# Key products of two 512-column matmuls per channel chunk, with both PSUM banks for one half and the sum taken by VectorE into SBUF

## What is computed

```python
xn = group_norm(x)                                  # 32 groups, no affine part
q, k, v = split(xn_tokens @ qkv_w.T + qkv_b)        # 256 columns each
q = relu(q)
k = relu(k + pos_enc)                               # the part that the change touches
z  = 1 / (q . sum_over_tokens(k) + 1e-6)            # per head, 8 heads of 32
out = ((q @ (k.T @ v)) * z) @ proj_w.T + proj_b     # linear attention, per head
y = x + out
```

## Time and profile before

| | us |
|---|---|
| median of 3 executions | 2671.64 (2662.23 to 2674.28) |
| the profiled execution's own time | 2664.9 |
| its span, first to last instruction | 2663.1 |
| mean granted TensorE clock | 0.998 of full speed |

### The profile page before, as it was taken

The page is one execution under the profiler, slowest core; times in us unless marked ns, Lnnn a source line. Parts: engine busy times, 40 slices in busy tenths (PEclk is TensorE's granted clock), DMA queues, the critical chain, the costliest instruction groups (busy, mean ns, idle before and its releaser), DMA issues.

```text
span 2663.1 us, 45248 instructions
## 1 busy us (share of the span) xinstructions
PE 2595.4 (97%) x15812; PEld 2215.1 (83%) x15812; DVE 1590.4 (60%) x2500; ACT 1660.0 (62%) x2543; POOL 1955.2 (73%) x1217
## 2 busy tenths in 40 slices
PE   5999999999999999999999999999999999999997
PEld 4878888788888888888888888888888888888885
DVE  6646666566665565656566555566655666555546
ACT  4656666565666656666666665666666666665654
POOL 4758777686777867767687786877768687686875
PEclk9999999999999999999999999999999999999999
DMA  7557878787787878878788687887878788776769
GB/s 260 180 181 229 273 226 267 218 262 237 237 266 226 266 225 248 254 244 250 237 270 257 210 262 237 252 263 225 254 243 254 235 264 250 238 237 200 229 184 296
DMA packets 357472, 642.07 MB, mean 241 GB/s; under 512 B 34432, under 2 KB 55808, under 8 KB 357248
## 3 DMA queue, kind: packets, MB, share of 16 engines
q1 hardware_dynamic: 357248, 639.18, 77.3%
HBM read 519.25 MB, written 119.80 MB: 240 GB/s over the span
## 4 chain that ended last, share of the span: by engine, by line
PE 74%; DVE 6%; issue 6%; POOL 6%; ACT 4%; DMA 3%; SPq 1%; ACTq 0%; DVEq 0%; POOLq 0%
PE banks L549 17%; PE banks L573 16%; PE banks L605 15%; PE banks L561 11%; PE banks L563 5%; PE banks L540 5%; PE banks L590 3%; POOL kacc L1229 2%; POOL hl L1215 2%; DMA y<-xr 2%; ACT xn L1015 2%; DVE kk L840 1%; DVE banks L835 1%; DVE stats L819 1%; POOL posb L1236 1%
## 5 line engine op out<-in xcount | busy, mean ns | idle before, releaser
L1229 POOL TENSOR_TENSOR kacc<-kacc,kt 128x512 f32<-128x512 f32 x368 | 476.2, 1294 | 307.2 <-ACT kt L1044 304.9
L549 PE MATMUL banks<-wqk,hl 128*128 128x256 f32 x4608 | 646.1, 290 | 12.8 <-POOL hl L1215 12.7
L1215 POOL TENSOR_TENSOR hl<-xn,hl 128x512 fp32r<-128x512 f32 x384 | 494.6, 1309 | 207.5 <-ACT hl L1027 207.3
L825 DVE TENSOR_TENSOR xt<-banks,xt 128x512 fp32r<-128x512 f32 x400 | 274.5, 686 | 569.1 <-ACT xt L1032 568.9
L573 PE MATMUL banks<-hl,wqk 128*128 128x512 f32 x2304 | 600.7, 396 | 6.5 <-DVE xr L854 6.4
L549 PEld LDWEIGHTS banks<-wqk,hl 128*128 128x128 f32 x4608 | 575.6, 191 | 18.6 <-POOL hl L1215 18.6
L561 PE MATMUL banks<-kk,xt 128*128 128x512 f32 x1600 | 584.8, 400 | 3.6 <-DVE kk L840 3.6
L605 PE MATMUL banks<-uhl,mhl 128*128 128x512 f32 (+1 forms) x2316 | 541.7, 383 | 2.1 <-DVE xr L854 2.1
L1244 POOL TENSOR_TENSOR q<-q,zb 128x1024 f32<-128x1024 f32 x180 | 432.9, 2405 | 113.7 <-DMA zb<-z_rows 113.5
L605 PEld LDWEIGHTS banks<-uhl,mhl 128*128 128x128 f32 x2316 | 423.7, 188 | 89.8 <-issue 2.5
L573 PEld LDWEIGHTS banks<-hl,wqk 128*128 128x128 f32 x2304 | 406.3, 188 | 100.3 <-DVE xr L854 8.7
(11 more groups left out here) (117 smaller groups left out, 2374.2 us busy)
## 6 DMA issues: line engine op xcount, KB each, us to landing
posb<-pos_plus_bk SPq DMA_DIRECT2D x375, 256.0 KB, 5.7
xs<-in_x SPq DMA_DIRECT2D x184, 512.0 KB, 6.0
xa<-in_x SPq DMA_DIRECT2D x184, 512.0 KB, 6.4
xr<-in_x SPq DMA_DIRECT2D x184, 512.0 KB, 3.9
zb<-z_rows SPq DMA_DIRECT2D x736, 128.0 KB, 4.5
y<-xr SPq DMA_DIRECT2D x184, 512.0 KB, 7.2
z_rows<-zt SPq DMA_DIRECT2D x32, 256.0 KB, 5.5
posb<-in_pos SPq DMA_DIRECT2D x25, 256.0 KB, 4.2
```

Of the source, the lines that this page charges most:

```text
L549: last = mm(psK[:, par(n, h), i * C:(i + 1) * C], hl_of(t)[:, a, c, s:s + P], wqk[:, w, c, C:2 * C], start=(j == 0), stop=(j == len(terms) ...
L1215: g.tensor_tensor(hl_of(t)[:, 1, :, s], xn_of(n, t)[:, :, s], hl_of(t)[:, 0, :, s], ALU.subtract).then_inc(xl_ready, 1)
L1229: g.tensor_tensor(both, both, kt[:, par(n, h), :], ALU.add).then_inc(ks_done, 1)
```

## The change

The two key products that share a stationary operand (high x by high weights, high x by low weights) become one matmul: its moving operand is the high and the low weights of the keys side by side, 2 x 256 columns, and its output fills a whole bank. The third product (low x by high weights) is added into the bank's first 256 columns. Each of a half's two tiles so takes one bank, and a half takes both; the keys of a half therefore wait for `kt_ready` of the half before in place of `kr_ready` of the half two before. VectorE adds the bank's second part and the position into `kt`, and then the bank's first part to that, also into `kt`; the second addition waits for the first through the new semaphore `kp_ready`, the first waits for `ks_done` of the half two before, since `kt` is written earlier than it was. `key_high`, `key_low` and `key_keep` read `kt` in SBUF in place of PSUM, and `key_keep` works in place.

```diff
@@ transpose_and_k
-                wait(pe, kr_ready, half_no(n, h) - 2)
+                wait(pe, kt_ready, half_no(n, h) - 1)
                 for i in range(TILES):
                     s = tok + i * P
-                    terms = [(c, a, w) for c in range(CC) for a, w in ((0, 0), (0, 1), (1, 0))]
-                    for j, (c, a, w) in enumerate(terms):
-                        last = mm(psK[:, par(n, h), i * C:(i + 1) * C], hl_of(t)[:, a, c, s:s + P], wqk[:, w, c, C:2 * C],
-                                  start=(j == 0), stop=(j == len(terms) - 1))
+                    for c in range(CC):
+
+                        mm(psK[:, i, :].rearrange("p (w n) -> p w n", w=2), hl_of(t)[:, 0, c, s:s + P], wqk[:, :, c, C:2 * C],
+                           start=(c == 0), stop=False)
+                        last = mm(psK[:, i, 0:C], hl_of(t)[:, 1, c, s:s + P], wqk[:, 0, c, C:2 * C],
+                                  start=False, stop=(c == CC - 1))
@@ key_add
-                v.tensor_tensor(psK[:, par(n, h), :], psK[:, par(n, h), :], posb[:, s, :], ALU.add).then_inc(kt_ready, 1)
+                wait(dve, ks_done, half_no(n, h) - 2)
+                both = kt[:, par(n, h), :].rearrange("p (i n) -> p i n", i=TILES)
+                v.tensor_tensor(both, psK[:, :, C:2 * C], posb[:, s, :].rearrange("p (i n) -> p i n", i=TILES),
+                                ALU.add).then_inc(kp_ready, 1)
+                dve.wait_ge(kp_ready, half_no(n, h))
+                v.tensor_tensor(both, psK[:, :, 0:C], both, ALU.add).then_inc(kt_ready, 1)
@@ key_low
-                v.scalar_tensor_tensor(out=kk[:, hp, :, 1, :], in0=psK[:, hp, :].rearrange("p (i n) -> p i n", i=TILES),
+                v.scalar_tensor_tensor(out=kk[:, hp, :, 1, :], in0=kt[:, hp, :].rearrange("p (i n) -> p i n", i=TILES),
                                        scalar=0.0, in1=kk[:, hp, :, 0, :].bitcast(F32),
                                        op0=ALU.max, op1=ALU.subtract).then_inc(kl_ready, 1)
@@ key_high
-                a(kk[:, par(n, h), :, 0, :], psK[:, par(n, h), :].rearrange("p (i n) -> p i n", i=TILES),
+                a(kk[:, par(n, h), :, 0, :], kt[:, par(n, h), :].rearrange("p (i n) -> p i n", i=TILES),
                   ACT.Relu).then_inc(kh_ready, 1)
@@ key_keep
-                wait(act, ks_done, half_no(n, h) - 2)
                 act.wait_ge(kl_ready, half_no(n, h))
-                a(kt[:, par(n, h), :], psK[:, par(n, h), :], ACT.Relu).then_inc(kr_ready, 1)
+                a(kt[:, par(n, h), :], kt[:, par(n, h), :], ACT.Relu).then_inc(kr_ready, 1)
```

More of the change, by code:

```diff
@@ L139, in build @@
         xtl_ready = sem("xtl_ready")
+        kp_ready = sem("kp_ready")
         kt_ready = sem("kt_ready")
```

## The result

The changed kernel takes 3040.88 us (median of 4, 3035.64 to 3042.38) against 2670.45 us of the kernel before (median of 4): ratio 1.139, 95% interval 1.137 to 1.141. It is slower by 370 us. The forecast was 3089 us with a range of 2890 to 3345. The profiled execution took 3040.5 us, its span is 3038.5 us.

What follows compares the result with a forecast made beforehand. PE at 97% was taken as the bound, with the ACT-DVE loop 0.78 us behind in a 12.10 us step. Summed, 292 + 301 + 16 - 129 - 56 = 424 us on 2664.9 gave 3089 us, range 2890 to 3345.

Steps and rivals of the forecast that it cites:

- The loop: Closed chain of ACT's and DVE's in-order lists through one step: 12.10 us with 0.78 to spare, predicted to become 14.4.
- The second addition: On DVE, in the chain in both halves: 0.73 us each, 400 times, 292 us.
- The wait for POOL: Odd half's key_low, with two SBUF inputs, waits until POOL's u_low ends: 1.57 us, 192 times, 301 us.
- ACT's reads of SBUF: ACT's copies of 512 elements from SBUF instead of PSUM: 0.02 us more, 800 times, 16 us.
- The cover: Existing waits that absorb added time: ACT's 128.9 us for PE's queries, and 56 us at the 15 batch junctions.
- the two junction waits: Two operations at batch junctions waiting for PE, 62.0 and 44.9 us in all; 56 of the 107 were to absorb added time.
- PE, 36 us: Key matmuls on PE: a half's keys fall from 1.51 to 1.42 us, 0.09 less, 36 us for 400 halves.
- the first rival: PE stays the bound and gets faster, 2629 us, chance 0.04; or no change within 0.5%, chance 0.02.
- Signs: Expected in the trace: PE's share near 83%, 2.5 us of PE waiting a step, keys 1.42 us a half, steps 14.4 us.
- The addition alone: Rival: key_low does not wait for POOL, so only the second addition costs; 2811 us, chance 0.11.
- The wait in the even half: Rival: even half's key_low also waits, for POOL's scale, 250 us more; 3339 us, chance 0.08.

Runs made afterwards that it cites:

- e1_add: Kernel before with the addition of position and bias done twice in PSUM, the second waiting for the first; 2824.34 us, ratio 1.0577.
- e8_all: Changed kernel with POOL's scale and u_low waiting for key_low, statistics moved behind key_low, second query part's save moved behind x_high_t; 2792.59 us, ratio 1.0460.
- e2_sbuf: Kernel before with its one addition writing to kt in SBUF, which key_high, key_low and key_keep read; 2868.25 us, ratio 1.0744.
- e4_ulow: Changed kernel with POOL's u_low moved behind the key_sum of the odd half; 3044.06 us, ratio 1.1402.
- e6_gate: Changed kernel with two more POOL waits: scale for the even half's key_low, u_low for the odd half's; 2909.93 us, ratio 1.0899.
- e3_psum: Changed kernel with the sum written back to PSUM and read there, keys waiting for key_keep of the half before; 2932.63 us, ratio 1.0983.
- e5_mm: Kernel before with the new key matmuls alone, both tiles into the half's one bank, one addition, no new wait; 2651.84 us, ratio 0.9934.

## Why the prediction was right, and where its sizes were off

**The loop.** Right. PE was the bound by 0.78 us in 12.10, and the change put more than that on the chain of ACT and DVE beside it. The step came out at 14.29 for 14.43. That the chain is what counts is shown by e1_add (0.72 a step in each half, and no more than that, gives 12.82), and by e8_all, which shortens the chain to 11.86, keeps the additions, and has PE as the bound again in those steps.

**The second addition, 0.73 us.** 0.71 (1567.34 - 1566.63).

**The wait for POOL, 1.57 us in each odd half.** The mechanism, the half, the instruction of POOL and the 0.55 us behind its end are all as forecast, and e2_sbuf, e4_ulow and e6_gate show that it takes POOL's instruction and not the operands alone; e3_psum shows that it takes both inputs in SBUF. The size in sum was 301 us; `key_low`'s busy time grew by 400 x (1318 - 682) ns, 254 us (682 is its mean on the page of before). 165 of the 192 odd halves met `u_low`; those near junctions and in the first batch met other work or none, and 19 even halves waited that were to go free.

**ACT's reads of SBUF, 16 us.** 400 x (631 - 598) + 400 x (632 - 596) ns = 28 us, the means on both pages; the copy that I took for a measure was 0.614.

**The cover, 129 + 56 us.** ACT's query waits were used up but for 17.1 us. Of the two junction waits one fell by 42 us and the other not at all (44.9 and 47.3), and for the addition alone there was none (e1_add). With 0.71 x 400 = 284, 254 and 28 us added and 112 + 42 taken off the sum would be 412; 376 were measured between the two profiled executions. The 36 us between are not placed; some of `key_low`'s waits may lie outside the loop. That the sum came as near as 424 to 376 is in part luck: the wait for POOL was taken 47 us too high, while ACT's reads and the two covers together came out 43 us dearer than forecast.

**PE, 36 us.** This figure failed, though it is in the first rival's price and not in the sum, and the time did not hang on it. I took the gram for the model of the new keys; keys follow transposes, and the first matmul behind those costs 0.08 us more than the ones behind it, in both kernels. The whole gain is 17.8 us (e5_mm). The Trainium skill's spacing rule (TensorE: Matmul & The Clock Gate, Back-to-back issue gap) gave an estimate of 4 us; the measurement lies between the two.

**Signs.** PE's share was to be near 83% and is 88%, because its busy time rose from 2595.4 to 2672.4 us with 1600 fewer matmuls: the profile's matmuls overlap less when there are gaps between groups, and PE stands idle before 426 matmuls in place of 42. I should not have divided busy time by a new span. The step shown has 1.80 us of idle PE and not 2.5, 1.32 of it at the odd half's gram. The keys were to take 1.42 us a half and take 1.49. The rest of the signs came.

**The rivals.** PE did not stay the bound. The addition alone was to give 2811, and e1_add, which is that without ACT's 16 us, gives 2824. The wait in the even half came in 19 of 208 halves of the changed kernel, not as the rule; in e2_sbuf it came in 99 of them, in e4_ulow in 165.

## What to carry to other kernels

An engine at 97% is a bound only until the next chain is longer: before work is moved to an engine with 40% idle time, follow that engine's list through one full step, back to itself, and see how much of the period is waiting for the bound engine. Here that was 0.78 of 12.10 us, and the price was 1.4 us of additions plus a wait. And an operand moved from PSUM to SBUF can change who an instruction waits for: a VectorE instruction with two SBUF inputs here waited out whatever GpSimd had begun, so ask what that is at the moment when it comes.

## What was not expected of the hardware

POOL waits for DVE just as DVE waits for POOL: in e2_sbuf `u_low` takes 2.94 us in place of 2.39 when `key_low` begins 0.02 us ahead of it. So a collision avoided in one half was paid in the next, and the kernel with no second addition at all still lost 7.4%. And two added waits (e6_gate) made the kernel 131 us faster: `key_low` never got past a POOL instruction that had begun (191 times in the changed kernel), while one that has not begun can be held back at little cost.

A wait of PE can cost twice. In e8_all PE stands idle for 3.4 us at most junctions, and at 12 of the 14 its next matmuls then run longer, at a granted clock of 0.50 in the one shown; in the changed kernel it waits 0.8 to 0.9 us in the same place, and the six matmuls behind it take 1.49 to 1.52 us.
